# A new order of steps in a five-stage attention and feed-forward kernel: the first attention's turn and opening, and three of the four joins

## The chip, the cores and the metric

The kernel runs on one core of a Trainium2 chip. The metric is the device time of one execution in microseconds (us), lower is better; a kernel's number is the median of its runs. A core has five engines that run side by side, each its own list of instructions in order: TensorE (PE, matmuls and transposes; PEld is its weight load), VectorE (DVE), ScalarE (ACT), GpSimd (POOL) and SyncE (SP), which here issues most DMA transfers. They wait for one another through semaphores. TensorE runs at one of two clock levels, 1.2 or 2.4 GHz; the profile shows the granted share of the full level.

## The reference

The input is 8 sequences of 512 tokens with 256 numbers each.

```python
x = L0_attn_x                                                   # (8, 512, 256)
x = layernorm(x + first_attention(x))                           # no scale and shift
x = layernorm(x + ffn(x))

def first_attention(x):        # 16 heads of 16
    q, k, v = heads(split(x @ w_qkv + b_qkv))
    a = softmax((q @ k.T + causal_mask) / sqrt(16))
    return (a @ v) @ w_out + b_out

def ffn(x):                    # two layers, each:
    h = shift_token(x)                                          # half of the channels from the token before
    q, k, v = heads(split(h @ wqkv))                            # 8 heads of 64
    q, k = rotary_xpos(l2norm(q) * q_scale, l2norm(k) * k_scale)
    x = x + local_attention(q, k, v) @ wo                       # windows of 128, one window back
    h = layernorm(shift_token(x)) * ln_g + ln_b
    a, g = split(h @ w1 + b1)                                   # 2 x 682
    x = x + (a * gelu(g)) @ w2 + b2
```

## The kernel before

The program has five stages one after another: the first attention, then twice a local attention (with its output projection) and a feed-forward. Each stage goes over the 8 sequences; 512 tokens of one sequence are four tiles of 128 rows. Matrices that need more than one pass of TensorE are split into a high and a low part (`_hi`, `_lo`), so a product is three matmuls per 128 rows of depth (L554 to L556).

**Steps and turns.** The order of all work is written out by hand, as lists of steps such as `st:11`. `follow` (L119) walks one list on every engine, and each engine does only its own part of a step, so a list sets the order within each engine; across engines only semaphores hold. A stage is a loop of seven turns over its `STEPS`. A step named `f_...` works ahead, for the next sequence; the others finish the current one. Before the first stage stands an `OPENING`; between two stages stands a list in `JOINS`, which finishes the last sequence of one stage together with the first front steps (`+...`) of the next. Join 0 goes from the first attention to local attention 0, join 1 to feed-forward 0, join 2 to local attention 1, join 3 to feed-forward 1; the fifth list ends the program.

**Steps of the first attention.** Heads go in pairs, p = 0 to 7, and in four groups of four heads (two pairs).
- `f_x` loads the next sequence (SP, L298) and transposes it (PE, L576); `f_xe` splits it (ACT L410, DVE L474).
- `f_qk:0` to `3` are the projections to q and k, 128 columns each (PE, L554 to L556); `f_qe:i` takes them out (ACT L422, L426; POOL L371 for the low part) and stores them to `qk_parts` in DRAM (SP, L304 twice and L306, 256 KB each).
- `f_load:g` brings group g's rows back in a stacked layout, to `a_Q` and `a_K` (SP, L322, four transfers of 192 KB). It waits for the stores of `f_qe:0` and `1` (g = 0, 1) or `2` and `3` (g = 2, 3), and until the current sequence has done with that group (`sc_full`).
- `sm:i` (and `f_sm:i`), i = 4p + q: scores of a pair of heads for one tile of 128 queries with the mask added (PE, L631, L637), then their maximum on DVE (L491). Two PSUM banks take turns, so TensorE's sm:i waits for the maximum of sm:i-2.
- `mt:g` turns the maxima of a group (PE L663, ACT L445) and sends them by two small DMAs into a row of `a_Q` (SP, L327), where they are subtracted by the next product. The st steps of a group wait for them (`m_in`): st:0, 6, 12 and 18.
- `st:i`, i = 3p + t: the scores transposed, keys on partitions, in three parts of 512, 384 and 384 columns (PE L676, L681), and their exponential (ACT, L454); `ms` masks the diagonal (POOL, L379).
- `pv:g` is the product with V and, by a column of ones, the sums (PE, L704, 32 matmuls). `z0` turns the result (DVE L510) and takes the reciprocal (L512), `z1` scales it (DVE L516) and splits it (POOL L384, L386; for z1:3 DVE L522, L524), `z2` turns it back (DVE L529), `z3` rounds it (ACT L435).
- `xr` loads x again and adds the bias (POOL L367, DVE L502); `out:t` is the output product for one tile (PE L720, L722), the sum with x and its statistics (DVE L536, L539, L543); `f_v` are the values (PE, DVE L497); `end` normalises and stores (ACT L440, POOL L398).

**Local attention and feed-forward.** Here the names mean the same, with other lines: scores and maxima L1176 and L1077, transposed scores and exponential L1210 and L991, turned q and k `f_t` (PE L1151, after POOL's L914), `set:0` four memsets on DVE (L1033 to L1036), `w1`, `h`, `w2` and `y` the feed-forward's products. `nx`, `rl`, `nw` and `nwo` are early loads of the next stage's data by SP (nw:0 in the opening: two transfers of 768 KB, L753, and eight of zero rows, L178). `ns:n` splits the next stage's weights: in join 3 ACT's L1345 rounds half of the 128 x 2 x 1364 numbers of w1, and DVE's L1357 takes the rest; `f_n` there is the statistics of the feed-forward's input (DVE L1554, L1557).

```python
for n, stage in enumerate(stages):
    with eng.Fori(0, NB - 1) as it:
        for step in stage.steps:
            do[n](*step, it + (stage.base + 1) if step in stage.ahead else it + stage.base)
    for name, i in joins[n]: ...
```

Of the kernel before, what the change touches and what calls it, by code (L numbers as in the profile page):

```python
# [183 lines left out]
def first_attention(nc, ctx, K, at, banks, scr, w, xin, rows_out, zeros, ahead, x, w_qkv, b_qkv, w_out, b_out, dst):  # L184
# [79 lines left out]
    STEPS = parse("""
        f_x:0 f_xe:0 st:8 sm:27 sm:28 mt:2 st:9 xr:0 f_qe:0 f_qk:0 f_qe:1 f_load:0 st:10 sm:29 f_qk:1 sm:30
        f_qk:2 ms:2 sm:31 st:11 ms:3 z0:0 pv:0 f_qe:2 mt:3 st:12 f_qe:3 z1:0 f_qk:3 st:13 pv:1 f_sm:0 st:14
        f_sm:1 f_sm:2 st:15 f_sm:3 ms:4 st:16 z2:0 f_sm:4 f_sm:5 z0:1 st:17 ms:5 f_sm:6 st:18 f_sm:7 st:19
        f_sm:8 z1:1 st:20 f_load:1 f_sm:9 f_sm:10 st:21 f_sm:11 f_mt:0 f_load:2 st:22 f_sm:12 f_sm:13 ms:6
        f_sm:14 st:23 pv:2 z3:0 f_st:0 z2:1 z0:2 ms:7 f_load:3 z1:2 f_sm:15 z0:3 pv:3 z3:1 f_sm:16 z2:2 f_st:1
        f_v:0 f_ms:0 z1:3 f_st:2 z3:2 f_mt:1 z2:3 f_sm:17 f_v:1 f_sm:18 f_v:2 z3:3 f_st:3 f_sm:19 out:0  # L270
        f_sm:20 f_st:4 out:1 f_sm:21 f_st:5 out:2 out:3 f_st:6 f_ms:1 f_sm:22 f_sm:23 f_st:7 f_v:3 f_sm:24
        f_sm:25 f_sm:26 end:0""")
# [1 line left out]
    OPENING = parse("""
        f_xe:0 f_x:0 f_qe:0 f_qk:0 f_qk:1 f_qk:2 f_qe:1 f_qk:3 f_qe:2 f_sm:0 f_sm:1 f_sm:2 f_load:0 f_sm:3
        f_sm:4 f_load:1 f_sm:5 f_sm:6 f_qe:3 f_sm:7 f_sm:8 f_sm:9 f_mt:0 f_sm:10 f_sm:11 f_load:2 f_sm:12
        f_v:0 f_st:0 f_load:3 f_sm:13 f_sm:14 f_sm:15 f_st:1 f_sm:16 f_st:2 f_ms:0 f_sm:17 f_sm:18 nw:0 f_st:3
        f_mt:1 f_st:4 f_sm:19 f_ms:1 f_sm:20 f_st:5 f_v:1 f_v:2 f_sm:21 f_sm:22 f_st:6 f_sm:23 f_sm:24 f_v:3
        f_sm:25 f_st:7 f_sm:26""")
# [1432 lines left out]

JOINS = [
    parse("""
        st:8 mt:2 sm:27 st:9 sm:28 sm:29 ms:2 ns:0 ns:1 st:10 pv:0 sm:30 +rl:0 st:11 st:12 ms:3 sm:31 st:13
        nx:0 z0:0 st:14 xr:0 z1:0 mt:3 +edge:0 st:15 +f_xe:0 ms:4 +f_x:0 z2:0 z0:1 st:16 +rot:0 pv:1 z1:1
        st:17 st:18 +f_qe:0 +f_qk:0 ms:5 st:19 z3:0 +f_qk:1 +f_qe:1 st:20 +f_iv:0 ms:6 +f_qe:2 ms:7 +f_qk:2
        z2:1 st:21 +f_qe:3 +f_qk:3 st:22 pv:2 z0:2 z1:2 +f_iv:1 st:23 +f_qe:4 +f_qk:4 +f_qe:5 z0:3 +f_qk:5
        z3:1 z2:2 +f_iv:2 pv:3 +f_qk:6 z1:3 +f_qk:7 +f_qe:6 z3:2 z2:3 +f_qe:7 out:0 +set:0 out:1 z3:3 out:2
        +f_iv:3 +f_te:0 +f_t:0 out:3 +f_te:1 +f_t:1 +f_sm:0 +f_t:2 +f_te:2 +f_sm:1 +pick:0 +f_t:3 end:0 nwo:0  # L1720
        +f_te:3 +f_sm:2 +f_v:0 +f_v:1 +f_v:2 +f_sm:3 ns:2 +f_v:3 +banks:0 +f_mt:0"""),
# [5 lines left out]
    parse("""
        +rot:0 ns:0 +rl:0 +edge:0 w1:2 nx:0 ns:1 h:2 w1:3 +f_xe:0 h:3 +f_x:0 w1:4 w1:5 +f_qk:0 +f_qk:1 h:4
        +f_qe:0 +tab:0 xr:0 +f_qe:1 +f_iv:0 +f_qe:2 +f_qe:3 fin:0 w2:0 +f_iv:1 +f_qe:4 +f_qe:5 +f_qk:2 +f_qk:3
        w2:1 +f_qk:4 +f_qk:5 +f_qk:6 +f_qk:7 +f_iv:2 +f_qe:6 w2:2 w2:3 +f_qe:7 h:5 w2:4 w2:5 +f_iv:3 +f_t:0  # L1730
        +f_t:1 +set:0 +f_te:0 y:0 +f_sm:0 +f_te:1 +f_sm:1 +f_t:2 nwo:0 +f_te:2 +f_sm:2 +f_te:3 +pick:0
        +banks:0 +f_t:3 +f_sm:3 +f_v:0 +f_v:1 ns:2 +f_v:2 +f_v:3 +f_mt:0"""),
# [84 lines left out]
```

## Time and profile before

| | us |
|---|---|
| runs | 1794.73, 1795.65, 1807.06 |
| median | 1795.65 |
| the profiled execution | 1800.07 |
| its span | 1798.5 |

| stretch of the profiled span | us |
|---|---|
| opening | 0 to 58.34 |
| seven turns of the first attention | 58.34 to 453.30 |
| join 0 | 453.30 to 519.68 |
| join 2 | 1117.85 to 1171.47 |
| join 3 | 1547.80 to 1607.05 |

TensorE is busy 95% of the span, DVE 64%, ACT 56%, POOL 48%; its mean granted clock is 0.958. A turn of local attention takes 53.7 to 53.9 us, one of the feed-forward 24.4 to 24.8. The boundaries are the starts of TensorE's first transpose for a new sequence.

In a row of the timeline one engine's neighbouring instructions of one kind stand together: start, time, engine, line, operation, out<-in, count, and in brackets how long the engine had stood idle before, and the instruction that ended it. DMA issues stand on SP's queue (SPq) at their issue; when the data is there is told by who waits.

### The profile page before, as it was taken

What the parts mean: (1) busy time and instruction counts of PE and PEld (TensorE: products, weight loads), DVE (VectorE), ACT (ScalarE), POOL (GpSimd) and SP (SyncE); (2) the same over time, 40 slices, a digit from 0 to 9 for tenths busy, and PEclk for the clock granted to TensorE, in tenths of its full rate; (3) what the DMA queues carried; (4) which work ended last, traced back from release to release, by engine and by line L of the source; (5) the groups of instructions that cost most, each with busy time, mean ns of one, the idle gap of its engine ahead of it and who ended that gap; (6) DMA issues with size and microseconds to landing.
All of it is one profiled execution on the core that took longest, in us unless ns stands there. A gap on an engine that the chain in (4) does not pass through costs nothing. (4 is left out here: it accounts for less than half of the span.)

```text
span 1798.5 us, 42022 instructions
## 1 busy us (share of the span) xinstructions
...
## 2 busy tenths in 40 slices
...
GB/s 178 175 121 119 159 158 146 132 109 146 49 60 36 1 34 35 35 35 24 15 81 105 70 61 81 48 13 35 35 35 35 0 35 23 84 61 91 93 82 47
DMA packets 102327, 129.64 MB, mean 72 GB/s; under 512 B 15834, under 2 KB 70788, under 8 KB 102276
## 3 DMA queue, kind: packets, MB, share of 16 engines
...
## 5 line engine op out<-in xcount | busy, mean ns | idle before, releaser
L454 ACT ACTIVATE a_PT<-b 128x384 f32<-128x384 f32 (+1 forms) x384 | 183.5, 523 | 132.7 <-PE b L676 77.3
L491 DVE TENSOR_REDUCE a_negm<-d 128x2 f32<-128x256 f32 (+3 forms) x256 | 201.7, 813 | 63.3 <-PE d L637 60.7
L907 POOL TENSOR_TENSOR l_t<-l_t,l_t 128x512 f32<-128x512 f32 x128 | 165.3, 1297 | 113.8 <-DVE l_t L1059 113.6
L1077 DVE CUSTOM_DVE_ANT_0 d<-d,window 128x256 f32<-128x256 f32 (+1 forms) x512 | 184.0, 420 | 22.8 <-PE d L1176 22.5
L991 ACT ACTIVATE l_PT<-b 128x512 f32<-128x512 f32 (+1 forms) x256 | 125.4, 542 | 100.9 <-PE b L1218 98.9
L1476 POOL TENSOR_TENSOR m_hid_lo<-m_hid,m_hid_hi 128x512 fp32r<-128x512 f32 x80 | 103.4, 1302 | 160.9 <-ACT m_hid_hi L1537 160.8
L921 POOL TENSOR_TENSOR l_PS<-l_PT 128x768 f32<-128x768 f32 x64 | 117.6, 1838 | 117.5 <-ACT l_PT L991 117.5
L1104 PE MATMUL d<-w,l_xt 128*128 128x512 f32 x384 | 164.6, 429 | 2.2 <-DVE l_t L1059 2.2
L379 POOL TENSOR_SCALAR_AFFINE_SELECT a_PT<-a_PT 128x512 f32<-128x512 f32 x128 | 79.8, 648 | 157.9 <-ACT a_PT L454 157.9
L1105 PE MATMUL d<-w,l_xt 128*128 128x512 f32 x384 | 152.0, 396 | 0.0
L1106 PE MATMUL d<-w,l_xt 128*128 128x512 f32 x384 | 151.6, 395 | 0.0
L631 PE MATMUL d<-a_K,a_Q 63*128 63x256 f32 (+2 forms) x512 | 122.3, 448 | 26.5 <-DMA a_K<-qk_parts 14.9
L1210 PE MATMUL b<-l_Q,l_K 64*128 64x256 f32 x1536 | 140.0, 295 | 4.3 <-ACT l_PT L991 3.1
L1210 PEld LDWEIGHTS b<-l_Q,l_K 64*128 64x128 f32 x1536 | 109.8, 188 | 42.5 <-ACT l_PT L991 19.3
L914 POOL TENSOR_TENSOR l_qk<-l_t,l_inv 128x512 f32<-128x512 f32 x128 | 131.5, 1051 | 0.0
L1235 PE MATMUL b<-l_PT,l_V 128*64 128x256 f32 (+1 forms) x1024 | 113.3, 364 | 2.1 <-ACT l_PT L991 1.4
L1577 DVE SCALAR_TENSOR_TENSOR m_hid<-b,mw_b,m_gate 128x512 f32<-128x512 f32 (+1 forms) x48 | 35.9, 748 | 122.9 <-ACT m_gate L1524 97.3
L954 ACT ACTIVATE l_sq<-d 128x512 f32<-128x512 f32 x128 | 76.7, 599 | 61.1 <-PE d L1106 44.8
L1054 DVE TENSOR_REDUCE l_ss<-l_sq 128x8 f32<-128x512 f32 x128 | 87.2, 681 | 33.7 <-ACT l_sq L954 33.2
L1094 DVE TENSOR_TENSOR rows_out<-b,l_xr 128x256 f32<-128x256 f32 x64 | 27.2, 425 | 123.6 <-PE b L1106 123.6
L1537 ACT ACTIVATE m_hid_hi<-m_hid 128x512 fp32r<-128x512 f32 x96 | 60.5, 630 | 73.4 <-DVE m_hid L1577 73.3
L925 POOL TENSOR_TENSOR l_zl<-l_zt,l_zh 128x512 fp32r<-128x512 f32 x64 | 82.0, 1307 | 37.5 <-ACT l_zh L997 37.5
...
## 6 DMA issues: line engine op xcount, KB each, us to landing
...
```

The lines of the kernel that those rows point to most:

```text
L454: nc.scalar.activation(PT[:, p // PG % 2, 2 * (p % PG) + hh, QOFF[t]:QOFF[t] + nq], SC[hh][:, 0:nq], ACT.Exp, scale=AD ** -0.5).then_inc(e ...
L491: dve.tensor_reduce(negm[:, q, 2 * p:2 * p + 2], MX[i % 2][:, :, 0:nk], AX.X, ALU.max, negate=True).then_inc(max_done, 1)
L631: pe.matmul(bank[:, hh, 0:nk], Q[rows, p, P * q:P * q + P], Kk[rows, p, 0:nk], start=True, stop=True)
L907: pool.tensor_tensor(t1[:, par, w, :], t1[:, par, w, :], t2[:, par, w, :], ALU.add)\
L914: pool.tensor_tensor(qk[:, i, w, :].rearrange("p (h d) -> p h d", d=FD), t1[:, par, w, :].rearrange("p (h d) -> p h d", d=FD), inv[:, par, ...
L921: pool.tensor_tensor(PS[:, i % 2], PT[:, i % 2, :, 1:TB, 0:P], PT[:, i % 2, :, 0:TB - 1, P:2 * P], ALU.add).then_inc(ps_done, 1)
L991: nc.scalar.activation(PT[:, p % 2, hh, j:j + 2, :].rearrange("p j q -> p (j q)")[:, 0:nq], SC[hh][:, 0:nq], ACT.Exp, scale=8.0).then_inc( ...
L1077: m = dve.tensor_tensor_reduce(out=o, in0=o, in1=mask, scale=-1.0, scalar=-NEG, op0=ALU.add, op1=ALU.min, accum_out=negm[:, q + t, p // 2, ...
L1104: pe.matmul(o, a_hi, r_hi, start=first, stop=False)
L1105: pe.matmul(o, a_lo, r_hi, start=False, stop=False)
L1106: return pe.matmul(o, a_hi, r_lo, start=False, stop=last)
L1210: pe.matmul(SC[hh][:, 2 * P * t:2 * P * t + 2 * P], lhs, rhs, start=(t == 0 and n == 0), stop=False, skip_group_check=True)
```

## The change

Five lists of steps are written in another order: the first attention's `STEPS` and `OPENING`, and the lists of joins 0, 2 and 3. No step is added or removed, no instruction, tile, semaphore or transfer is another. The lists of local attention and feed-forward, join 1 and the end stay. Of the diff, the head of the turn's list and of join 3:

```diff
@@ -262,21 +262,21 @@
     STEPS = parse("""
-        f_x:0 f_xe:0 st:8 sm:27 sm:28 mt:2 st:9 xr:0 f_qe:0 f_qk:0 f_qe:1 f_load:0 st:10 sm:29 f_qk:1 sm:30
+        f_xe:0 f_x:0 sm:27 st:8 sm:28 xr:0 mt:2 st:9 f_qe:0 f_qk:0 f_qk:1 f_qe:1 st:10 sm:29 ms:2 f_qk:2 ms:3
...
@@ -1712,28 +1712,28 @@
 JOINS = [
...
     parse("""
-        nx:0 sm:4 st:0 +f_n:0 st:1 sm:5 nz:0 ns:0 ps:0 pv:0 sm:6 st:2 sv:0 sm:7 z:0 ps:1 st:3 ps:2 mt:1 zs:0
+        sm:4 st:0 sm:5 nz:0 st:1 ps:0 sm:6 ps:1 st:2 sm:7 ns:0 pv:0 sv:0 z:0 zn:0 st:3 +f_n:0 mt:1 pv:1 ns:1
```

Engine by engine, what moves in the first attention's turn:
- PE: f_qk:1 stands directly behind f_qk:0 (st:10 and sm:29 stood between them); st:11 goes ahead of sm:31, st:12 ahead of mt:3; sm:27 ahead of st:8; f_mt:0 goes behind st:22, f_sm:12 ahead of it; f_sm:14 behind pv:2; f_sm:16 from behind pv:3 to behind f_mt:1; out:0 and out:1 stand together, out:2 and out:3 too, with f_sm:20 and f_st:4 between the two pairs; f_v:3 behind f_sm:24.
- DVE: z2:0 from behind f_sm:3 to behind f_sm:8; z0:1 from behind f_sm:5 to behind f_sm:11; z1:1 from behind f_sm:8 to behind f_sm:12; z2:1 and z0:2 ahead of f_sm:14; out as on PE.
- ACT: st:12 ahead of mt:3, st:22 ahead of f_mt:0, z3:0 ahead of st:23. POOL: ms:6 ahead of z1:1. SP: f_load:1 directly behind f_load:0.

In the turn on SP, the stores of f_qe:2 (L304, L306), f_qe:3's and mt:3's small transfers (L327) now stand behind f_load:1's four transfers; before, f_load:1 came after all of them:

```order
 L322 DMA a_K<-qk_parts 48x2x512
+L315 ISA
+L322 ISA
+L322 DMA a_Q<-qk_parts 48x2x512
+L322 ISA
+L322 DMA a_Q<-qk_parts 48x2x512
+L322 ISA
+L322 DMA a_K<-qk_parts 48x2x512
+L322 ISA
+L322 DMA a_K<-qk_parts 48x2x512
 L301 REGISTER_ALU
 L304 ISA
```

The first row is the last transfer of f_load:0, the last two are the beginning of f_qe:2's stores; L315 is f_load:1's wait.

In the turn on DVE, the place of z2:0 (L529), whose row now stands behind five more maxima (L491):

```order
 L491 TENSOR_REDUCE a_negm<-d 128x2
+L490 REGISTER_ALU
+L491 TENSOR_REDUCE a_negm<-d 128x2
+L490 REGISTER_ALU
+L491 TENSOR_REDUCE a_negm<-d 128x2
+L490 REGISTER_ALU
+L491 TENSOR_REDUCE a_negm<-d 128x2
+L490 REGISTER_ALU
+L491 TENSOR_REDUCE a_negm<-d 128x2
+L490 REGISTER_ALU
+L491 TENSOR_REDUCE a_negm<-d 128x2
 L527 REGISTER_ALU
```

The row ahead of the five is the maximum of f_sm:3, the last one that of f_sm:8; L527 begins z2:0.

In join 3 on DVE, before: f_n's statistics stand ahead of sm:5's maxima (L1077), and the first product for the weights (L1357, ns:0) ahead of those of sm:6 and sm:7:

```order
 L1554 BN_STATS m_st<-xin 128x6 x4
 L1557 BN_AGGR m_mv<-m_st 128x2 x4
 L1077 ISA d,l_negm<-d,window 128x256
 L1077 ISA l_negm 128x1
 L1077 ISA d,l_negm<-d,window 128x256
 L1077 ISA l_negm 128x1
 L1077 ISA d,l_negm<-d,window 128x256
 L1077 ISA l_negm 128x1
 L1077 ISA d,l_negm<-d,window 128x256
 L1077 ISA l_negm 128x1
 L1357 TENSOR_TENSOR w_54<-mw_w_raw,w_53 128x1364
 L1077 ISA d,l_negm<-d,window 128x128
```

and in the changed list, where sm:7's last maximum goes ahead of both:

```order
 L1077 ISA d,l_negm<-d,window 128x256
 L1077 ISA l_negm 128x1
 L1357 TENSOR_TENSOR w_54<-mw_w_raw,w_53 128x1364
 L1086 TENSOR_TENSOR l_zt<-b,l_rr 128x512
 L1554 BN_STATS m_st<-xin 128x6 x4
 L1557 BN_AGGR m_mv<-m_st 128x2 x4
 L1357 TENSOR_TENSOR w_54<-mw_w_raw,w_53 128x1364
```

Here all eight pairs of L1077 rows of sm:6 and sm:7 have moved ahead of L1357 and of L1554. On ACT the first L1345 goes behind st:2 and the second ahead of st:4; POOL and TensorE follow the same list.

In the opening, nw:0's loads and zero rows go to the front of SP's list, f_load:0 ahead of f_qe:2's stores, f_load:1 behind f_qe:3's, f_load:3 ahead of f_mt:0 and f_load:2 behind it. In join 0, rl:0 (SP) goes later, xr:0 on DVE from ahead of z1:0 to behind z0:1, and set:0 ahead of out:0. In join 2, set:0 goes ahead of f_qe:0 on DVE and y:0 ahead of f_te:0, and w2:1 to w2:5 on TensorE all stand behind f_qk:7 (w2:1 stood behind f_qk:3).

## Rows read from the trace of the kernel before

**Rows 1.** Windows: stretch, us, busy PE, PEld, DVE, ACT, POOL, clock, DMA, GB/s.

```profile
58.34:118.59 60.25, 56.97 (x492) 37.18 (x489) 41.23 (x71) 34.90 (x71) 19.87 (x30) 0.83 0.40 115
...
174.05:231.13 57.08, 55.21 (x489) 35.13 (x489) 40.37 (x70) 34.87 (x71) 21.90 (x32) 0.88 0.49 138
231.13:286.55 55.42, 53.26 (x489) 33.35 (x489) 40.39 (x70) 34.74 (x71) 21.80 (x32) 0.94 0.51 143
...
1547.80:1607.05 59.25, 50.60 (x449) 39.78 (x449) 23.96 (x68) 31.94 (x54) 22.57 (x25) 0.94 0.33 99
```

**Rows 2.** Timeline of TensorE in the turn from 231.13: sm:31, st:11, f_sm:0, st:18.

```profile
240.42 0.50 PE L631 MATMUL d<-a_K,a_Q 63*128 63x512 f32 x2 [0.39 <-DVE a_negm L491]
...
240.83 0.49 PE L681 MATMUL b<-a_Q,a_K 64*128 64x256 f32 x4
...
249.36 0.39 PE L631 MATMUL d<-a_K,a_Q 63*128 63x256 f32 x2 [0.54 <-DMA a_K<-qk_parts]
...
254.55 0.88 PE L676 MATMUL b<-a_Q,a_K 64*128 64x512 f32 x2
```

**Rows 3.** Windows of shorter stretches, in that turn, the opening and join 3.

```profile
253.00:260.00 7.00, 6.48 (x59) 4.21 (x60) 6.97 (x13) 5.21 (x11) 3.59 (x6) 0.93 0.33 68
...
243.30:249.20 5.90, 5.52 (x58) 2.65 (x50) 1.40 (x3) 3.65 (x8) 3.15 (x4) 1.00 0.85 204
...
253.00:256.70 3.70, 3.27 (x26) 1.91 (x26) 3.67 (x8) 2.77 (x7) 2.45 (x4) 1.00 0.63 130
...
18.00:20.00 2.00, 0.00 (x0) 0.00 (x0) 0.44 (x1) 1.72 (x3) 1.59 (x2) 1.00 1.02 378
...
1559.50:1566.30 6.80, 5.58 (x40) 4.32 (x42) 3.35 (x17) 2.81 (x7) 1.64 (x1) 0.50 0.33 81
```

**Rows 4.** Part 5 of the page: busy us, mean ns; idle before, releaser.

```profile
L491 DVE TENSOR_REDUCE a_negm<-d 128x2 f32<-128x256 f32 (+3 forms) x256 | 201.7, 813 | 63.3 <-PE d L637 60.7
```

**Rows 5.** Timeline of DVE in the same turn: z2:0, z0:1, z2:1, z0:2, z0:3, out.

```profile
253.06 0.70 DVE L529 STREAM_TRANSPOSE a_ztf<-a_on 128x512 f32<-128x512 f32 x1
...
254.59 0.70 DVE L510 STREAM_TRANSPOSE a_ot<-b 128x512 f32<-128x512 f32 x1
255.32 0.25 DVE L512 RECIPROCAL a_rc<-a_ot 128x16 f32<-128x16 f32 x1
...
264.96 0.71 DVE L529 STREAM_TRANSPOSE a_ztf<-a_on 128x512 f32<-128x512 f32 x1 [1.11 <-ACT a_zt L435]
267.01 0.72 DVE L510 STREAM_TRANSPOSE a_ot<-b 128x512 f32<-128x512 f32 x1 [1.35 <-PE b L704]
...
270.04 0.72 DVE L510 STREAM_TRANSPOSE a_ot<-b 128x512 f32<-128x512 f32 x1 [0.42 <-PE b L704]
...
278.94 0.42 DVE L536 TENSOR_TENSOR a_y<-b,a_xr 128x256 f32<-128x256 f32 x1 [0.39 <-PE b L722]
...
280.80 0.42 DVE L536 TENSOR_TENSOR a_y<-b,a_xr 128x256 f32<-128x256 f32 x1 [0.38 <-PE b L722]
```

**Rows 6.** Timelines of join 3: DVE ns:0, ACT ns:0, TensorE sm:6.

```profile
1557.81 1.58 DVE L1357 TENSOR_TENSOR w<-mw_w_raw,w 128x1364 fp32r<-128x1364 f32 x1 [3.56 <-ACT w L1345]
...
1556.44 1.34 ACT L1345 ACTIVATE w<-mw_w_raw 128x1364 fp32r<-128x1364 f32 x1 [3.35 <-DMA mw_w_raw<-in_L_ffn_w]
...
1560.72 0.80 PE L1176 MATMUL d<-l_K,l_Q 64*128 64x256 f32 x4 [2.96 <-DVE l_negm L1077]
```

**Rows 7.** Timeline of SP in the same turn: issue of f_load:0's first transfers.

```profile
243.31 0.89 SPq L322 DMA_DIRECT2D a_Q<-qk_parts  x2
```

**Rows 8.** One line's instructions (z1:3): ns least, median, most; first and last start.

```profile
L522 DVE CAST a_on<-a_zn x8: 293/294/1236, 104.6 to 491.8; 128x256 fp32r<-128x256 f32 x8
```

**Rows 9.** Timeline of TensorE: opening f_sm:0, join 0 out:0, join 2 f_t:0.

```profile
26.41 0.58 PE L631 MATMUL d<-a_K,a_Q 63*128 63x256 f32 x2 [8.94 <-DMA a_K<-qk_parts]
...
497.43 0.58 PE L720 MATMUL b<-a_wo_hi,a_zt 128*128 128x256 f32 x1 [6.07 <-ACT a_zt L435]
...
1152.55 1.09 PE L1151 MATMUL d<-ident,l_qk 128*128 128x128 f32 x8 [1.31 <-POOL l_qk L914]
```

More of the change, by code:

```diff
@@ L264, in first_attention @@
     STEPS = parse("""
-        f_x:0 f_xe:0 st:8 sm:27 sm:28 mt:2 st:9 xr:0 f_qe:0 f_qk:0 f_qe:1 f_load:0 st:10 sm:29 f_qk:1 sm:30
[L266 to L269, printed above, removed]
@@ L270, in first_attention @@
-        f_v:0 f_ms:0 z1:3 f_st:2 z3:2 f_mt:1 z2:3 f_sm:17 f_v:1 f_sm:18 f_v:2 z3:3 f_st:3 f_sm:19 out:0
-        f_sm:20 f_st:4 out:1 f_sm:21 f_st:5 out:2 out:3 f_st:6 f_ms:1 f_sm:22 f_sm:23 f_st:7 f_v:3 f_sm:24
-        f_sm:25 f_sm:26 end:0""")
+        f_xe:0 f_x:0 sm:27 st:8 sm:28 xr:0 mt:2 st:9 f_qe:0 f_qk:0 f_qk:1 f_qe:1 st:10 sm:29 ms:2 f_qk:2 ms:3
+        f_load:0 sm:30 f_load:1 st:11 sm:31 f_qe:2 pv:0 st:12 z0:0 mt:3 f_qe:3 z1:0 f_qk:3 st:13 pv:1 f_sm:0
+        st:14 f_sm:1 f_sm:2 st:15 f_sm:3 st:16 f_sm:4 st:17 f_sm:5 f_sm:6 st:18 f_sm:7 st:19 ms:4 f_sm:8 st:20
@@ L273, in first_attention @@
+        z2:0 f_sm:9 f_sm:10 st:21 f_sm:11 ms:5 z0:1 ms:6 f_sm:12 st:22 z1:1 f_mt:0 f_sm:13 z3:0 st:23 z2:1
+        pv:2 z0:2 f_sm:14 ms:7 z1:2 f_st:0 f_ms:0 f_load:2 f_load:3 f_sm:15 z0:3 pv:3 z3:1 z2:2 f_st:1 f_v:0
+        z1:3 f_st:2 z3:2 f_mt:1 f_sm:16 z2:3 f_sm:17 f_st:3 f_v:1 f_sm:18 f_v:2 z3:3 f_sm:19 out:0 out:1
+        f_sm:20 f_st:4 out:2 out:3 f_st:5 f_ms:1 f_sm:21 f_sm:22 f_st:6 f_sm:23 f_st:7 end:0 f_sm:24 f_v:3
+        f_sm:25 f_sm:26""")
     FIRST = [s for s in STEPS if s[0][0] == "f"]
@@ L274, in first_attention @@
     OPENING = parse("""
[L275 to L279, printed above, removed]
+        f_x:0 f_qk:0 nw:0 f_xe:0 f_qk:1 f_qk:2 f_qe:0 f_qk:3 f_qe:1 f_load:0 f_sm:0 f_sm:1 f_sm:2 f_sm:3
@@ L281, in sync @@
+        f_qe:2 f_sm:4 f_sm:5 f_sm:6 f_qe:3 f_sm:7 f_load:1 f_load:3 f_sm:8 f_sm:9 f_sm:10 f_mt:0 f_ms:0
+        f_sm:11 f_sm:12 f_v:0 f_sm:13 f_sm:14 f_st:0 f_sm:15 f_load:2 f_st:1 f_sm:16 f_sm:17 f_st:2 f_sm:18
+        f_sm:19 f_mt:1 f_sm:20 f_st:3 f_sm:21 f_v:1 f_st:4 f_v:2 f_st:5 f_sm:22 f_sm:23 f_v:3 f_ms:1 f_st:6
+        f_sm:24 f_sm:25 f_st:7 f_sm:26""")
     def sync(sp):
@@ L1714 @@
     parse("""
[L1715 to L1721, printed above, removed]
+        st:8 mt:2 sm:27 nx:0 st:9 sm:28 sm:29 ns:0 st:10 ms:2 pv:0 ms:3 st:11 sm:30 sm:31 ns:1 +edge:0 st:12
+        mt:3 z0:0 st:13 +f_x:0 st:14 z1:0 st:15 +f_xe:0 pv:1 z2:0 z0:1 xr:0 st:16 z1:1 ms:4 st:17 ms:5 +rot:0
+        st:18 +f_qk:0 +f_qe:0 st:19 +f_qk:1 +f_qe:1 ms:6 ms:7 st:20 z3:0 z2:1 st:21 z0:2 +f_qk:2 +f_iv:0 st:22
+        z1:2 +f_qe:2 pv:2 +rl:0 st:23 +f_qk:3 +f_qe:3 z0:3 z3:1 +f_iv:1 pv:3 +f_qk:4 z2:2 +f_qe:4 +f_qe:5 z1:3
+        z3:2 +f_iv:2 +f_qe:6 z2:3 +f_qk:5 +f_qe:7 +set:0 +f_qk:6 z3:3 +f_qk:7 out:0 +f_iv:3 out:1 out:2
+        +f_te:0 +f_t:0 out:3 +f_t:1 +f_te:1 +f_sm:0 +f_t:2 +f_te:2 +f_sm:1 nwo:0 end:0 +pick:0 +f_te:3 ns:2
+        +f_t:3 +f_sm:2 +f_v:0 +f_v:1 +f_sm:3 +banks:0 +f_v:2 +f_v:3 +f_mt:0"""),
     parse("""
```

14 lines of the change are left out of this document (7 added, 7 removed).

## Prediction

> **What bounds the kernel now.** I read the windows by stage first, then the timelines of the stretches that the change touches, and last the DMA rows. The reader is to see three things.
>
> First, the sizes [rows 1]. An undisturbed first-attention turn takes 55.42 us and TensorE is busy in 53.26 of them, so all its waits together are about 2 us, and only a part of those can be won by order. There are seven such turns, so 1 us in a turn is 7 us in the kernel. Turns also differ by their granted clock: 57.08 us at a mean of 0.88, 55.42 at 0.94, with the same work; in the records each turn runs some microseconds in its middle at the lower of two levels (1.2 instead of 2.4 GHz). That is worth 1.66 us, as much as all that an order could win, and it is not under the order's direct control.
>
> Second, what ends the waits in a turn [rows 2]. TensorE waits 0.39 us at sm:31 for a maximum on DVE, and 0.54 at f_sm:0 for the DMA that brings K of the next sequence. Where f_sm and st alternate, it follows DVE: there DVE is busy in 6.97 of 7.00 us [rows 3], since each score tile costs one maximum, 813 ns in the mean [rows 4]. Later DVE itself idles: 1.11 us before z2:1, 1.35 before z0:2, 0.42 before z0:3. At the turn's end it waits 0.39 and 0.38 for the out products on TensorE, two of the four [rows 5]; in the list f_sm:20 and f_st:4 stand between out:0 and out:1, and f_sm:21 and f_st:5 ahead of out:2.
>
> Third, join 3 [rows 6]: TensorE stands 2.96 us at sm:6, for a maximum that stands behind ns:0 on DVE, which waits for ACT's half of ns:0, which waits for the DMA of the feed-forward weights. Of the 59.25 us of this join [rows 1] it is the largest wait. Behind it 6.80 us run at a clock of 0.50 [rows 3].
>
> **The turn, part by part.** No instruction is added or removed, so all prices are waits.
>
> (a) f_qk:1 comes directly behind f_qk:0 on TensorE; st:10 and sm:29 stood between. So f_qe:1's stores leave earlier by about those two steps, some 0.7 us by my estimate (one score step takes 0.41, from 240.42 to 240.83 [rows 2]; an st step is of the same size), and so does f_load:0 behind them: the 0.54 at f_sm:0 goes. st:11 now stands ahead of sm:31 and covers part of its 0.39. Bounds 0 and -0.93 (both waits), I take **-0.7**, as the DMA wait is the larger and the surer.
>
> (b) z0:1 (0.70 + 0.25) leaves the stretch in which DVE is the limit [rows 3, 5]; z2:0 (0.70) moves only from behind f_sm:3 to behind f_sm:8, inside it. That is -0.95 if nothing else waits. Something does: on SP, f_load:1 (four transfers of 192 KB) now goes ahead of f_qe:2's three stores (256 KB each) and of mt:3's two small ones, which bring the maxima for st:18. Ahead of mt:3's rows stand then f_load:0, f_load:1 and f_qe:2: three times 768 KB, 2.36 MB. In the profile f_load:0 is issued at 243.31 [rows 7], with (a) at 242.6. The stretch that carries f_load:0 and f_qe:2 now moves 204 GB/s [rows 3]: 11.6 us, so mt:3's rows land at 254.2. st:18 starts at 254.55 now [rows 2] and would, with (a) and without z2:0 ahead of it, start at 253.15. So it waits about 1.0 us. DVE has nearly one maximum (0.81) left to do when TensorE stops, so about 0.3 of it shows: **-0.65**. Bounds: by the rate of 378 GB/s that the opening's queue reaches [rows 3], no wait and -0.95, with z2:0's 0.70 won as well -1.65; by 130 GB/s, the slowest loaded stretch [rows 3], the rows land at 260.8 and st:18 waits 7.6. I take 204, as that row holds the same kinds of transfers. f_load:1 itself is wanted only at f_sm:8 and is now early. f_qe:3's stores come later by f_load:1's transfers, but f_load:2, which waits for them, is issued far behind.
>
> (c) The steps that left (z0:1, z1:1, z2:1 and z0:2 behind f_sm:11 to f_sm:13) land where DVE idles 1.11, 1.35 and 0.42. I cost them at 0; the cover is 2.88 us against 0.95 moved in. If the cover is gone, the price is 0.95. ms:6 now goes ahead of z1:1 on POOL, which brings DVE's z1:1 beside a POOL instruction. What that can cost is seen in z1:3: the same cast takes 294 ns alone and 1236 in join 0, beside a busy POOL [rows 8]. So at most +0.94, also under the cover.
> The Trainium skill speaks against this place: "SBUF — State Buffer", section "Who interferes with whom", says that VectorE and GpSimd share one port pair and that a VectorE instruction with two SBUF inputs contends with a GpSimd instruction that reads SBUF; z1 is of that kind, affine_select as well. The 1236 ns agree with it. By the rule a turn would lose up to 0.94 and the sum be -12.4, 1783; by the idle rows it loses nothing.
>
> (d) out:0 and out:1 stand together on TensorE now, out:2 and out:3 too. DVE's two waits of 0.39 and 0.38 [rows 5] can go; the maxima that waited behind them come earlier, and f_sm:26 with them. Bounds 0 and -0.77; I take **-0.45**, a little over one of the two, because DVE must still do the same sequence at the end.
>
> A turn then wins 0.7 + 0.65 + 0.45 = 1.8, seven turns **-12.6**. The clock I cost at nothing, with 1.66 either way for a turn as its bound.
>
> **Opening.** TensorE waits 8.94 us at f_sm:0 for K [rows 9]. f_load:0 no longer stands behind f_qe:2's 768 KB, which take 2.0 us at 378 GB/s [rows 3]. Against that, 1.5 MB of later weights go to the front of the queue, where it is empty for about four microseconds before the first stores, and f_load:1 goes behind f_qe:3. Bounds -3 (the 2.0 and a shorter low-clock stretch) and +1.5 (the weights not done before the stores: 1.5 MB at 378 GB/s are 4.2 us). I take **-1**: half of the 2.0, since f_load:1 then limits.
>
> **Join 0.** TensorE waits 6.07 at out:0 for the last z3 [rows 9]. DVE's set:0 comes ahead of out:0 and xr later, both into that wait; the chain z1:3, z2:3, z3:3 keeps its neighbours on POOL. Bounds -3 (half the wait) and +2 (set:0 delays z2:3): **-1**. **Join 2.** f_t:0 waits 1.31 for POOL's chain [rows 9], which does the same work in the same order; set:0 and y:0 change places on DVE. Bounds -1.3 and +1.5: **0**.
>
> **Join 3.** ns:0 and f_n:0 go behind sm:7 on DVE, ACT's half behind st:2. The 2.96 us go in full, as the weights are there at 1556.4, where ACT's L1345 starts (1556.44) [rows 6], and nothing of sm and st needs them. Of the stretch at 0.50 that follows, TensorE is busy 5.58 us, work of 2.8 at full clock; I take half of the difference, 1.4, as some stretch at low clock follows in any case. **-4.4**; bounds -1.5 (half the wait comes back at st:3, behind ACT's 1.34 for ns:0) and -5.8 (2.96 + 2.8). DVE's product of 1.58 is late next, and only f_w1 wants it.
>
> **Sum.** -1 - 12.6 - 1 + 0 - 4.4 = -19.0. The profiled execution took 1800.07 us, which is 4.4 above the median of 1795.65; on it the forecast is 1781, on the median **1777**. The median is what the changed kernel's is compared with.
>
> **Rivals.**
> *The gains don't add* (chance 0.27). The z steps pay in their new place what they save in the old (the 0.94 of (c)), (a) and (d) turn into waits one step later, and the low clock fills what idle was won. The turn wins 0.8, the joins only the 2.96: -5.6 - 3 = -8.6, **1787**. For it: turns are 96% busy on TensorE, and the three waits at full clock are small. Against: the waits have different enders (DMA, DVE, TensorE), so one doesn't take the other's place.
> *st:18 is not late* (0.16). If mt:3's rows land by 253, at the upper rate, b gives -1.65, with (a) and (d) at their bounds -3.35 a turn: -23.5 - 4.4 - 2, **1766**.
> *st:18 stalls* (0.12): slower. The point is the rate at which 2.36 MB pass. At 165 GB/s the rows land at 256.9, st:18 waits 3.7, and the gain is gone: a turn at +0.9, seven times, eats the 6.4 of opening and joins. At 130 GB/s the wait of 7.6 makes a turn 4.8 longer: +33.6 - 6.4, **1823**; midway 1809. For it: 130 GB/s is a real row of this turn. Against: that stretch has only the load's own transfers, at a DMA share of 0.63 [rows 3], so the queue was not full.
> *The change does nothing* is excluded by the order; the same time by cancellation lies in the first rival.
>
> **Numbers.** The forecast has 0.45. A measurement of this kernel can't tell less than about 1% from no change: 1777.7 to 1813.6 counts as the same. The forecast lies on that border, with a spread of about 8 us from the bounds; I put 0.28 of its 0.45 below. With the second rival: faster 0.44. The first rival and the rest of the forecast, and half the third: 0.27 + 0.17 + 0.06 = same 0.50. Slower 0.06. The range from 1764 to 1796 leaves out the third rival nearly whole and the lower part of the second.
>
> **What would show it.** In the changed profile: the wait at f_sm:0 gone; a wait for the DMA of mrow at st:18 of about 1 us (none: second rival; over 3.7: third); DVE's waits at out under 0.2; turns of 53.6 at a clock of 0.94; sm:6 of join 3 without a wait, that join near 55; f_sm:0 of the opening near 25. The forecast is wrong if the turns' mean clock falls, or if TensorE meets a new wait of over a microsecond at pv or out.

## The result and the profile after

The changed kernel takes 1787.41 us (median of 8 runs, 1782.39 to 1791.96) against 1800.39 (8 runs of the kernel before, 1794.73 to 1807.06): a ratio of 0.9934, 95% interval 0.9913 to 0.9955. That is 12 us less (8 to 16). Forecast were 19 us less, 1777 on a median of 1795.65. The direction was right, the size 1.6 times the measured.

The profiled execution of the changed kernel took 1787.27 us, its span is 1785.7. Of its stretches, the opening, the first, fourth and fifth turn, join 0 from its st:8, join 2 and join 3 (windows; columns as in [rows 1]):

```profile
0.00:56.05 56.05, 37.03 (x246) 25.59 (x246) 35.58 (x41) 18.57 (x32) 20.11 (x34) 0.73 0.62 189
56.05:114.92 58.87, 55.13 (x491) 36.84 (x489) 40.73 (x69) 34.44 (x70) 19.93 (x30) 0.86 0.47 127
...
226.93:279.33 52.40, 50.43 (x488) 33.25 (x489) 40.59 (x70) 34.45 (x71) 22.46 (x32) 1.00 0.52 151
279.33:336.43 57.10, 54.94 (x489) 35.74 (x489) 40.89 (x70) 34.73 (x71) 22.45 (x32) 0.88 0.51 138
...
444.23:515.43 71.20, 58.70 (x380) 38.84 (x379) 57.32 (x125) 39.09 (x81) 35.08 (x48) 0.88 0.21 61
1101.11:1165.41 64.30, 57.58 (x326) 46.58 (x325) 47.35 (x107) 34.14 (x59) 29.70 (x32) 1.00 0.20 59
1517.50:1594.35 76.85, 72.32 (x649) 57.44 (x646) 37.94 (x114) 45.32 (x79) 31.28 (x31) 1.00 0.26 77
```

The same cuts of join 0 (from its st:8), join 2 and join 3 (each with the part of the turn ahead of it) in the kernel before:

```profile
452.98:519.68 66.70, 55.26 (x380) 36.21 (x379) 55.25 (x125) 40.59 (x82) 35.06 (x49) 0.92 0.21 65
1104.71:1171.47 66.76, 60.76 (x325) 49.92 (x324) 47.94 (x107) 34.04 (x59) 29.74 (x32) 0.92 0.15 49
1523.65:1607.05 83.40, 74.75 (x648) 59.20 (x645) 37.68 (x114) 45.44 (x79) 30.87 (x31) 0.96 0.24 71
```

| term | forecast | these two profiles |
|---|---|---|
| opening | -1 | -2.3 |
| seven turns (394.64 to 388.18) | -12.6 | -6.5 |
| join 0 | -1 | +4.5 |
| join 2 | 0 | -2.5, at a clock of 1.00 against 0.92 |
| join 3 | -4.4 | -6.5, at 1.00 against 0.96 |
| all that was not changed | 0 | +0.6 |
| sum | -19.0 | -12.7 |

Two things stand out. Join 0 is longer, in these two profiles by more than the bounds that were given. Part of that is chance of the execution: over the profiles of all kernels here, this stretch lasts 66.7 to 69.3 us with the old list (mean 68.1, five profiles) and 68.8 to 71.2 with the new one as it stands (mean 69.6, five). And the wait that term (a) was to take away is larger, not gone (timeline of TensorE, f_sm:0 of two turns, then st:18; [rows 2] has 0.54 and none):

```profile
188.98 0.38 PE L631 MATMUL d<-a_K,a_Q 63*128 63x256 f32 x2 [1.00 <-DMA a_K<-qk_parts]
...
298.34 0.38 PE L631 MATMUL d<-a_K,a_Q 63*128 63x256 f32 x2 [1.43 <-DMA a_K<-qk_parts]
...
194.55 0.50 PE L676 MATMUL b<-a_Q,a_K 64*128 64x512 f32 x2 [0.52 <-DMA a_Q<-a_mrow]
```

The 0.52 is the wait for mt:3's rows that step (b) foretold; it stands in one turn of seven.

In join 3 the wait that was forecast to go is gone. (The 2.96 us of [rows 6], which the rows and the prediction call sm:6's, stand at sm:7, the fourth score product of this join, which waits for sm:6's maxima on DVE.) sm:7 has no wait left, DVE's L1357 comes after it and waits 0.68, and ACT's L1345 finds the weights all but there (0.20 us against 3.35 in [rows 6]):

```profile
1551.19 1.58 DVE L1357 TENSOR_TENSOR w<-mw_w_raw,w 128x1364 fp32r<-128x1364 f32 x1 [0.68 <-ACT w L1345]
...
1549.82 1.34 ACT L1345 ACTIVATE w<-mw_w_raw 128x1364 fp32r<-128x1364 f32 x1 [0.20 <-DMA mw_w_raw<-in_L_ffn_w]
```

### The profile page after: what moved, and what is told of

Read it like the earlier page. It is cut to its first block, busy times and chain, and to the rows that moved or that the text cites. A ratio compares the mean times of both kernels' runs of the same rounds, so it can differ in the third digit from the quotient of the medians.

```text
span 1785.7 us, 42024 instructions
## 1 busy us (share of the span) xinstructions
PE 1704.7 (95%) x13984; PEld 1305.2 (73%) x13984; DVE 1150.5 (64%) x2853; ACT 997.9 (56%) x1927; POOL 866.6 (49%) x886
## 4 chain that ended last, share of the span: by engine, by line
PE 81%; DVE 6%; DMA 4%; issue 3%; ACT 3%; POOL 1%; SPq 1%; DVEq 0%; POOLq 0%; ACTq 0%
PE b L1210 8%; PE d L1104 6%; PE b L1235 6%; PE d L1105 5%; PE d L1106 5%; PE d L631 3%; PE d L1151 3%; PE b L676 3%; PE d L1176 3%; PE b L704 3%; PE d L1623 2%; PE d L1625 2%; PE d L1624 2%; PE b L1250 2%; DMA a_K<-qk_parts 2%
## 5 line engine op out<-in xcount | busy, mean ns | idle before, releaser
L491 DVE TENSOR_REDUCE a_negm<-d 128x2 f32<-128x256 f32 (+3 forms) x256 | 201.1, 814 | 67.1 <-PE d L637 65.3
L1077 DVE CUSTOM_DVE_ANT_0 d<-d,window 128x256 f32<-128x256 f32 (+1 forms) x512 | 184.4, 422 | 24.9 <-PE d L1176 24.6
L631 PE MATMUL d<-a_K,a_Q 63*128 63x256 f32 (+2 forms) x512 | 123.8, 449 | 24.3 <-DMA a_K<-qk_parts 18.0
```

The lines of the kernel that those rows point to most:

```text
L491: dve.tensor_reduce(negm[:, q, 2 * p:2 * p + 2], MX[i % 2][:, :, 0:nk], AX.X, ALU.max, negate=True).then_inc(max_done, 1)
L631: pe.matmul(bank[:, hh, 0:nk], Q[rows, p, P * q:P * q + P], Kk[rows, p, 0:nk], start=True, stop=True)
L1077: m = dve.tensor_tensor_reduce(out=o, in0=o, in1=mask, scale=-1.0, scalar=-NEG, op0=ALU.add, op1=ALU.min, accum_out=negm[:, q + t, p // 2, ...
```

## The experiments

Ratios are to the kernel before, run beside each kernel on the same chip. Times after f_x are counted from TensorE's first transpose of the same turn.

**One part alone.** The new turn without the rest, and the new join 3 without the rest:

```diff
 before.py with
+    STEPS = (the changed kernel's)            # e3
+    JOINS[3] = (the changed kernel's)         # e4
```

> The kernel before with the new turn alone. By the profile the seven turns win 6.5 us (394.6 to 388.2), less than the 12.6 forecast: ratio 0.9964, f_sm:0 still waits for K. If the forecast's price of the turn was right and that one execution unlucky with the clock, 0.993.

> The kernel before with the new join 3 alone. By the profile join 3 wins 6.5 us (ratio 0.9964): the 2.96 us at sm:6, some 1.2 at st:1 and st:5, and the stretch at the low clock behind them. If the clock's part was chance, 3 to 4 us (0.998). If the wait only moves to f_w1, nothing.

Measured: e3 0.9926 (0.9911 to 0.9941), of 1804.1 some 13 us (11 to 16); e4 0.9967 (0.9948 to 0.9985), 6 us (3 to 9). So over several runs the turn is worth what was forecast, 12.6, and not the 6.5 of the one profile. How it gets there is another matter. One turn of e4, which has the old order, passed wholly at full clock; beside it the turn of the changed kernel that did so too:

```profile
175.55:228.88 53.33, 50.51 (x488) 32.31 (x489) 40.26 (x70) 34.76 (x71) 21.96 (x32) 1.00 0.50 148
```

53.33 (e4) against 52.40 (changed): between these two turns the order wins 0.93 us, 6.5 in seven. Turns that spent the same time at 1.2 GHz say the same. Over turns two to six of all profiles, with 6.8 us at that level the old order takes 55.25 us in the mean (five turns) and the new 54.62 (eight); with 13.7 us it is 57.07 (six) against 55.77 (nine). That is 0.6 to 1.3 us in a turn, 4 to 9 in seven. The rest goes with the clock: the mean granted clock was 0.964 in e3's six runs, 0.958 in the twelve of before beside them, and within the runs of any one kernel 0.001 more clock goes with about 1.0 us less (least squares over all runs, each kernel from its own mean), which makes 6 us by this estimate.

In e4's execution the old join 3 is gone; e3's, which still has it, passed it at a clock of 1.00 (window of join 3, then TensorE's sm:7 in it):

```profile
1515.87:1596.95 81.08, 72.31 (x648) 57.43 (x645) 37.35 (x114) 45.48 (x79) 30.85 (x31) 1.00 0.25 73
...
1552.42 0.50 PE L1176 MATMUL d<-l_K,l_Q 64*128 64x256 f32 x4 [2.09 <-DVE l_negm L1077]
```

So at equal clock the new list (76.85) wins 4.2 there, and TensorE's idle time falls from 8.8 to 4.5 us. Of the 4.2, sm:7's wait is 2.09; the rest are smaller waits, such as st:1's, 1.23 and then 0.35. What the list wins beyond 4.2 goes with the clock: no profile with the new list, of eleven, has a low stretch in join 3, and two of the three with the old list have one.

**Join 0.** The old list in the changed kernel, and the new one in the kernel before:

```diff
 after.py with
+    JOINS[0] = (the kernel before's)          # e2
 before.py with
+    JOINS[0] = (the changed kernel's)         # g
```

> The changed kernel with the list of join 0 as it was before. Theory: the new join 0 costs 4.5 us (from its first st:8 to the next f_x 71.2 us against 66.7), so this kernel is 4.5 us faster than the changed one, near 0.991 of before, and out:0 waits about 6 us for z3 as before. Rival: the join is longer only because the clock fell in another place; then the time stays within 1 us of the changed kernel's.

> The kernel before with the new join 0 alone. Theory: slower by 2 to 5 us (ratio 1.001 to 1.003): rot:0 takes 3.18 us beside POOL instead of 1.50, f_qe's chain on DVE is 1 us longer by the wait for pv:2 at z0:2, and f_t:0 waits 1 us for out:2 behind set:0. Rival (the forecast): 1 us faster, 0.9994.

Measured: e2 0.9883 (0.9865 to 0.9901), so 9 us better than the changed kernel, with an uncertainty of 5. g 1.0015 (0.9995 to 1.0035), 2.7 us slower (-0.9 to 6.3). e2 shows that the new join costs time. How much is not settled: 9 us (4 to 14) by e2, 2.7 by g, whose interval just leaves out the forecast of 1 us less, and 1.5 by the mean of the profiles. In three places it shows new delays. DVE's rot:0, beside POOL's z1:1, ms:4 and ms:5 (timeline of DVE, changed kernel, then e2):

```profile
464.74 0.95 DVE L1018 TENSOR_TENSOR l_rots<-l_rots,l_scales 128x256 f32<-128x256 f32 x1
465.61 0.72 DVE L1020 SCALAR_TENSOR_TENSOR l_rots<-l_rots,l_scales 128x128 f32<-128x128 f32 x1
466.25 0.72 DVE L1023 TENSOR_TENSOR l_rots<-l_rots,l_scales 128x128 f32<-128x128 f32 x1
```

```profile
465.84 0.42 DVE L1018 TENSOR_TENSOR l_rots<-l_rots,l_scales 128x256 f32<-128x256 f32 x1
466.18 0.28 DVE L1020 SCALAR_TENSOR_TENSOR l_rots<-l_rots,l_scales 128x128 f32<-128x128 f32 x1
466.38 0.28 DVE L1023 TENSOR_TENSOR l_rots<-l_rots,l_scales 128x128 f32<-128x128 f32 x1
```

The whole of rot:0 takes 3.18 us instead of 1.50, on DVE, which is busy 57.32 of the 71.20 us here. Then DVE stands still before z0:2, because pv:2 comes late, and set:0's memsets come ahead of out:0's sum, whose end releases out:2, behind which f_t:0 stands on TensorE (changed kernel, DVE):

```profile
473.75 0.72 DVE L510 STREAM_TRANSPOSE a_ot<-b 128x512 f32<-128x512 f32 x1 [2.33 <-PE b L704]
...
492.46 0.91 DVE L1033 MEMSET l_negm<- 128x1024 f32 x1 [0.16 <-issue]
...
494.65 0.35 DVE L536 TENSOR_TENSOR a_y<-b,a_xr 128x256 f32<-128x256 f32 x1
```

out:2 starts at 495.06, POOL's last l_qk ends at 495.66, and f_t:0 starts at 496.93. These kernels mend the places:

```diff
 join 0 of after.py
-  ... out:0 +f_iv:3 ... with +set:0 ahead of +f_qk:6
+  ... out:3 +set:0 +f_t:1                                   # e7
-  mt:3 ... z0:1 xr:0 ... ms:5 +rot:0 ... pv:2 +rl:0
+  +rl:0 mt:3 ... z0:1 +rot:0 xr:0 ... ms:5 ... pv:2         # e8
   e8 and
-  z0:2 +f_qk:2 +f_iv:0 st:22 z1:2 +f_qe:2 pv:2
+  +f_qk:2 +f_iv:0 st:22 +f_qe:2 z0:2 z1:2 pv:2
+  out:0 +set:0 +f_iv:3                                      # h
```

> The changed kernel with set:0 behind out:3 in join 0. Theory: DVE's four memsets (2.27 us) ahead of out:0's sum hold out:2 and with it f_t:0 on TensorE for 1.07 us after POOL has its last l_qk; without them f_t:0 starts within 0.3 us of POOL's end, and join 0 is some 1 us shorter. Rival: f_t:0 waits for POOL alone; then the join stays near 71.

> The changed kernel with rl:0 ahead of mt:3 and rot:0 ahead of xr:0 in join 0. Theory: DVE's rot:0 takes 3.18 us there because it runs beside POOL's z1:1, ms:4 and ms:5 (1.50 in the kernel before, beside an idle POOL); moved ahead it takes 1.5, the first f_qe:0 on DVE starts 1.5 to 2.6 us earlier, and join 0 (69.5 to 71.2 us) comes 1.5 to 2.5 us nearer to the 66.7 to 69 of the old list. Rival: DVE waits for pv:2 at z0:2 anyway (2.3 us), so that the join stays.

> The changed kernel with three edits in the new list of join 0: rl:0 ahead of mt:3 and rot:0 ahead of xr:0 (as e8), z0:2 and z1:2 behind f_qe:2, set:0 back between out:0 and out:1. Theory: these three places are all that the new join loses: rot:0 takes 1.5 us, DVE doesn't stand still before z0:2, f_qe's chain on DVE from f_qe:0 to f_qe:7 takes 24.3 us as in the old list instead of 25.3, f_t:0 starts within 0.8 us of POOL's end, and the kernel stands where e2 stood, at 0.989 of before. Rival: the price of the new join lies elsewhere (mt:3's wait of 0.98 us, the place of the low clock); then the ratio stays at 0.993.

e7 missed: f_t:0 starts 0.63 us after POOL's end instead of 1.27, but the memsets are now late for f_t:2, and the join is 72.62:

```profile
501.48 0.45 PE L1151 MATMUL d<-ident,l_qk 128*128 128x128 f32 x1 [3.05 <-DVE l_Q L1065]
```

e8 did half: rot:0 takes 1.50, the first f_qe:0 on DVE no longer waits for DVE but for TensorE (2.35 us behind f_qk:0's start, as in the old list; 4.7 in the changed kernel). The join's length, 71.16, did not show it: in that execution TensorE ran at the low clock from 9.8 to 20.0 us after st:8, and f_qk:0 started at 22.0; in the changed kernel's the first low stretch lay from 18.9 to 22.4, and f_qk:0 started at 18.1. One execution cannot weigh 1.7 us against that. h, with all three places mended: 0.9923 (0.9897 to 0.9950). rot:0 takes 1.50, f_t:0 starts 0.06 us after POOL; but f_qe's chain takes 26.3 us, not 24.3, since DVE waits on (h, timeline of DVE, the first sum of f_qe:3):

```profile
476.97 0.69 DVE L1054 TENSOR_REDUCE l_ss<-l_sq 128x8 f32<-128x512 f32 x1 [2.11 <-ACT l_sq L954]
```

So the theory that these three places are the whole price fell; the rival's 0.993 lies in the interval and e2's 0.9883 does not. What h still has of the new list at that place is TensorE's order: f_qk:3 behind st:22, pv:2 (2.36 us) and st:23. In the old list it stands ahead of them, and in e2 DVE has no wait before f_qe:3 (0.48 before f_qe:2, 0.69 before f_qe:4). That this order is the rest of the price was not tried by itself, and stays open.

**Term (a): what holds f_load:0.** In the turn DVE's sum of x and bias (xr, L502) now runs beside POOL's low parts of f_qe:0 and f_qe:1; POOL takes 3.51 us for the two (changed kernel), and 2.53 when xr comes later (e1, the last row):

```profile
233.44 3.51 POOL L371 TENSOR_TENSOR a_qk_lo<-a_part_f,a_qk_hi 128x512 fp32r<-128x512 f32 x2 [3.29 <-ACT a_part_f L426]
...
233.91 1.90 DVE L502 TENSOR_TENSOR a_xr<-a_xr,a_bo 128x1024 f32<-128x1024 f32 x1 [2.91 <-DMA a_xr<-in_L_attn_x]
...
230.57 2.53 POOL L371 TENSOR_TENSOR a_qk_lo<-a_part_f,a_qk_hi 128x512 fp32r<-128x512 f32 x2 [3.30 <-ACT a_part_f L426]
```

The section "Who interferes with whom" of the Trainium skill's page "SBUF — State Buffer" describes such pairs: both of DVE's inputs in SBUF, POOL reading SBUF. Here and in rot:0 the trace agrees, with 2.25 us against 1.28 for one low part of POOL and 3.18 against 1.50 for rot:0. The next two kernels take that away, and then some of the traffic:

```diff
 e1:  the step's DVE part is named xb; POOL's load stays at xr
-        z1:0 f_qk:3
+        z1:0 xb:0 f_qk:3
 e5:  e1 and, in the stores of f_qe:0 and f_qe:1
+        n = 2 if i < 2 and slot and not isinstance(b, int) else S
+        sp.dma_start(scr[b, rows, slot, 0:n], qk_hi[:, i, 0:n].bitcast(F32))
+        (loads read scr[0])
```

> The changed kernel, but DVE's sum of x and the bias (xr, L502) stands behind z1:0 in the turn; POOL's load of x stays where it is. Theory: the gain of term (a) is lost because xr (1.90 us there) now runs beside POOL's low part of f_qe:1, which takes 2.25 us instead of 1.28. Then POOL's part ends 9.05 us after f_x instead of 10.0, f_load:0 is issued at 11.45 instead of 12.41, f_sm:0 starts at about 17.5 instead of 18.3 to 19.0, and a turn is 0.7 to 0.95 shorter: 5 to 6.5 us less than the changed kernel, a ratio to before of about 0.990. Rival: f_load:0 lands late because f_load:1's transfers share the queue with it; then its issue is earlier and f_sm:0 is not, and the ratio stays at 0.993.

> e1 with the second of the two high-part stores of f_qe:0 and f_qe:1 cut to two columns in the turns (512 KB less in front of f_load:0); it leaves out part of the data, and every sequence reads q and k of the first one. Theory: in e1 f_load:0 is issued no earlier than in the changed kernel (12.30 against 12.41 us after f_x) because the six stores of 256 KB pass the queue one per 0.68 us from 6.55 on, and the last lands at 12.1 whatever POOL does. With four of them the last one lands about 2.05 us after its issue at 9.5: f_load:0 at 11.75, f_sm:0 0.5 us earlier, near 17.8. Rival: f_load:0's wait is set by the latency of the last store alone; then its issue stays at 12.3.

e1: POOL takes 2.53 for both parts and ends 9.04 us after f_x, as expected, but f_load:0 is issued at 12.30 instead of 12.41, f_sm:0 starts at 18.15 to 18.59, and the ratio is 0.9934 (0.9917 to 0.9951), the same as the changed kernel's. The theory of POOL alone fell, and the rival as I had put it too (f_load:0's issue is not early). What e1 shows is a second bound of almost the same date, the queue: from 234.50 on the changed kernel's DMA moves 378 GB/s at a share of 1.02, all of it the six stores.

```profile
234.50:237.50 3.00, 2.71 (x28) 1.45 (x31) 3.00 (x4) 2.11 (x6) 3.00 (x4) 1.00 1.02 378
```

e5 lightens it by 512 KB for each sequence. It leaves out part of the stored data and reads every sequence's q and k from the first one's place, so only its times are of use. In it f_load:0 is issued at 11.80 after f_x, f_sm:0 starts at 17.7 to 18.1, and turns at full clock take 51.9 to 52.0 (SP, issue of f_load:0; e1's f_x at 224.06, e5's at 224.19):

```profile
236.36 0.35 SPq L322 DMA_DIRECT2D a_Q<-qk_parts  x1
```

```profile
236.00 0.35 SPq L323 DMA_DIRECT2D a_Q<-qk_parts  x1
```

Expected were 11.75 and 17.8. Some 0.2 us of what f_sm:0 wins there is not from the stores: with the fixed address the four transfers of f_load:0 are issued closer together, 1.34 us from first to fourth instead of 1.54.

So f_load:0 has two gates, POOL's second low part and the passage of six stores from the first one on. f_qk:1's new place moves the first: POOL's second low part ends 9.78 us after f_x in the kernel before and 9.04 in e1, which in the changed kernel xr took back. It does not move the second: f_qe:1's first store is issued 8.35 us after f_x in the kernel before and 8.59 in the changed one, since on SP it stands behind the store of f_qe:0's low part, which waits for POOL.

**Term (b): mt:3's rows.**

```diff
-        f_load:0 sm:30 f_load:1 st:11 ... mt:3 f_qe:3
+        f_load:0 sm:30 st:11 ... mt:3 f_load:1 f_qe:3      # e6
```

> The changed kernel with f_load:1 put behind mt:3's two small transfers on SP (still ahead of f_qe:3's stores). Theory: the wait of up to 0.52 us at st:18 for these rows goes in every turn, st:18 starts near 23.3 us after f_x in all turns instead of 23.3 to 24.4, and f_load:1 still lands by 24.3, in time for f_sm:8. Rival: f_load:1 then lands too late and the wait moves to f_sm:8.

No turn of e6 waits at st:18 or at f_sm:8; at full clock st:18 comes 4.72 to 4.73 us after f_sm:0, where the changed kernel's fourth turn has 4.95. One run: 1779.61 against 1803.21.

**Put together.** f1 is the changed kernel with the old join 0, xr's sum late and mt:3 ahead of f_load:1; f2 moves st:9 as well.

```diff
 f2 against f1
-        mt:2 st:9 f_qe:0 f_qk:0 f_qk:1 f_qe:1 st:10
+        mt:2 f_qe:0 f_qk:0 f_qk:1 f_qe:1 st:9 st:10
```

> The changed kernel with what the runs so far point to: the old list of join 0 (as e2), xr's sum on DVE behind z1:0 (as e1), and f_load:1 behind mt:3's small transfers (as e6). Theory: e2's ratio of 0.988, less 0.3 to 0.5 us in each turn: 0.986, about 25 us below before. Rival: the turn's gains are given back by the granted clock (e1's mean clock was 0.960 against 0.965 of the changed kernel); then 0.988 or more.

> f1 with st:9 behind f_qk:0, f_qk:1, f_qe:0 and f_qe:1 in the turn. Theory of the full queue: f_load:0 can only be issued when six stores of 256 KB have passed at 0.68 us each from the first one of f_qe:0; f_qk:0 starts 0.6 us earlier (2.65 us after f_x instead of 3.29), so f_load:0 is issued at 11.7 instead of 12.3, f_sm:0 starts near 17.7, and a turn is 0.5 us shorter than in f1: ratio 0.984. Rival: the exponentials that now come later (st:9, st:10) hold pv:0, and pv:1's end instead of f_load:0 sets f_sm:0; then no gain.

f1: 0.9881 (0.9853 to 0.9909), no better than e2 within its interval. f2: 1775.0, 0.9863 (0.9836 to 0.9891), better than the changed kernel, and by its median the fastest of all, though the intervals don't tell it from f1 and e2. It got there by neither theory: f_load:0 is issued at 11.6 to 12.0 as expected, but f_sm:0 starts at 18.7 to 20.3, against 17.9 to 18.3 in f1 (turns two to seven), since st:10 waits and pv:0 with it (the rival); yet the clock hardly falls (two of its turns, and st:10's wait):

```profile
111.76:164.51 52.75, 50.37 (x489) 33.08 (x489) 39.94 (x70) 34.70 (x71) 21.53 (x32) 1.00 0.52 150
164.51:218.74 54.23, 51.80 (x489) 33.99 (x489) 39.97 (x70) 34.76 (x71) 21.54 (x32) 0.97 0.51 146
...
226.30 0.44 PE L668 MATMUL b<-a_Q,a_K 64*128 64x384 f32 x1 [1.41 <-ACT a_PT L446]
```

## Why the prediction held in sign and not in size

The term with the wrong sign is **join 0**. I took -1 with bounds of -3 and +2; it measured +4.5 in the two profiles and +1.5 in the mean of all, 2.7 (-0.9 to 6.3) put in alone, and 9 (4 to 14) when taken out of the changed kernel. The sign is shown by the last; how the sizes go together stays open. I had seen that set:0 moves into out:0's wait and priced only that. I had not read what the moves put beside rot:0 on DVE: a neighbour on POOL (+1.7). The row of z1:3 [rows 8] showed the price of a busy POOL, and I used it for z1:1 alone. Nor had I costed what DVE waits for pv:2, 2.33 us before z0:2 in the changed kernel, or f_qk:3 behind pv:2 on TensorE, which in h holds f_qe:3 by 2.11 and was not tried by itself.

**The turn** was sized at -12.6, and measured 13 alone (11 to 16), but about half of that goes with the clock, which I had put at 0: that the total fits is luck. By order a turn wins 0.93 (0.6 to 1.3) and not 1.8. Part by part, at full clock on both sides (e4's third turn, the changed kernel's fourth; one turn of each, so a few tenths may be chance), against the forecast:
- (a) f_sm:0 starts 18.05 us after f_x in the old order, 18.31 in the new: +0.26 instead of -0.7. The premise was wrong. I took f_qe:1's stores to leave earlier with f_qk:1; its first store leaves 8.59 us after f_x instead of 8.35. What holds f_load:0 is six stores of 256 KB in a full queue, and POOL beside xr.
- (b) f_sm:0 to f_sm:13 takes 11.45 and 11.15: -0.3 instead of -0.65. The wait at st:18 exists, with 0.52 instead of 1.0 and in one turn of seven, and e6 removes it.
- (c) f_sm:13 to f_v:0 takes 7.81 and 7.24: -0.57 instead of 0. f_sm:16, which waits 0.69 for f_load:2 in that old turn, comes later now and doesn't wait; I had missed that move. The z steps cost nothing that shows in their new place, as put: beside POOL's mask z1:1 takes 0.48 instead of 0.41 in this turn and in the other at full clock, 0.67 to 0.68 in the five others, and z2:1 behind it waits for POOL anyway. The 1236 ns of [rows 8], which the prediction calls in agreement with a rule on two inputs, are of a cast, whose row has one; z1:1 itself has two, and it lost 0.07 to 0.27.
- (d) f_v:0 to the next f_x takes 16.02 and 15.70: -0.3 instead of -0.45. One of DVE's two waits at out is left, with 0.58.

**Opening** -2.3 instead of -1, within its bounds: f_sm:0 waits 7.88 us instead of 8.94 [rows 9] and starts 1.4 earlier. **Join 3** -4.2 at equal clock, and 6 (3 to 9) in runs, against -4.4: the wait at sm:7 went as put, but at equal clock it is 2.09 (e3), not 2.96. The rest are small waits that I had not listed, and what the clock gives. The 1.4 that I put for the low stretch is no part of the 4.2, so the size is right in part by luck. **Join 2** is 64.2 to 65.8 in the profiles with the new list and 66.2 to 66.8 in those with the old; the new ones also have the higher clock, so that the difference of the means, 1.6, is not split further.

**The rivals.** That gains don't add (1787) came out to the microsecond, by another mechanism: alone, the turn and join 3 win what was forecast (13 and 6), the clock gave rather than took, and join 0 took part of it back. At equal clock, though, a turn's 0.93 is near the 0.8 that this rival gave it. st:18 never stalled for long. The rate of 204 GB/s was right: in the turn that waits, 11.7 us pass from f_load:0's issue (182.84) to st:18 (194.55), against 11.6 put. But TensorE also came to st:18 later than put, as (a) won nothing.
